# Seventeen instead of nineteen destination buckets as dense products in the first two graph convolution passes

## The reference: what is computed

```python
x = x + gnn0(layernorm(x), src, dst, edge_weight)   # one weighted neighbour sum
x = x + experts(layernorm(x))                       # top 2 of 8 feed-forward experts
x = x + convolutions(layernorm(x), src, dst)        # three layers, below
x = x + slice_attention(layernorm(x))               # 8 heads, 64 slices

def convolutions(x, src, dst):
    row, col = src and dst with a loop at every node
    norm = dinv[row] * dinv[col]                    # dinv = 1/sqrt(degree)
    for i in range(3):
        h = x @ W[i]
        h = segment_sum(h[row] * norm[:, None], col, 6250) + b[i]
        x = relu(layernorm(h) * gamma[i] + beta[i])
    return x
```

## Time and profile before

| | |
|---|---|
| median of three runs | 4934.6 us (4934.17 to 4947.35) |
| the profiled execution | 4942.1 us, span 4940.4 us |
| PE, DVE, ACT, POOL busy | 74%, 38%, 19%, 59% of the span |
| stage 1 | 97 to 1290 us |
| expert blocks | 1381 to 2190 us, PE busy 787 of 809 |
| pass 1, pass 2 | 767 us each, PE busy 619 and 621 |
| pass 3 | 919 us, PE busy 712 |

### The profile page before, as it was taken

One profiled execution on the slowest core, in us unless ns is written; L12 is line 12 of the kernel. 1 busy time (PEld: TensorE's weight loads), 2 busy tenths in 40 slices (PEclk: granted clock), 3 DMA queues, 4 the chain that ended last, 5 costly groups with the idle time before them and its releaser, 6 DMA issues. The chain is left out here.

```text
span 4940.4 us, 53616 instructions
## 1 busy us (share of the span) xinstructions
PE 3646.7 (74%) x17389; PEld 2837.0 (57%) x17389; DVE 1858.6 (38%) x6845; ACT 922.3 (19%) x2129; POOL 2931.6 (59%) x2861
## 2 busy tenths in 40 slices
PE   1455555555699999976788887778788787877768
PEld 1344444444488888865566665557566555555547
DVE  4344443444711111125233333133333255555564
ACT  1233333333122222214000001000000011111120
POOL 4666666666467777751566665666666565656520
PEclk6677777777799999988899998889899798998888
DMA  5444444444166666666565556556567454555423
GB/s 157 146 163 155 143 152 158 152 141 135 23 185 196 183 195 184 190 178 209 164 187 176 181 178 203 163 170 186 174 183 221 145 164 150 153 159 156 143 95 141
DMA packets 431741, 807.47 MB, mean 163 GB/s; under 512 B 112299, under 2 KB 263250, under 8 KB 430738
## 3 DMA queue, kind: packets, MB, share of 16 engines
q1 hardware_dynamic: 264274, 465.45, 28.7%
q0 software_dynamic: 164064, 331.94, 24.6%
q10 hardware_dynamic: 3168, 7.21, 0.4%
HBM read 670.69 MB, written 133.67 MB: 163 GB/s over the span
## 5 line engine op out<-in xcount | busy, mean ns | idle before, releaser
L2544 POOL DMA_INDIRECT rows_h<-table,step_src x1522 | 1465.9, 963 | 1096.4 <-issue 547.3
L2584 PE MATMUL bank_g<-X,piece_h 128*128 128x256 f32 x5194 | 1240.4, 390 | 51.1 <-issue 36.9
L2584 PEld LDWEIGHTS bank_g<-X,piece_h 128*128 128x128 f32 x5194 | 1018.8, 197 | 240.5 <-issue 97.1
L892 POOL DMA_INDIRECT rows_r<-table,step_src x782 | 743.9, 951 | 402.2 <-issue 210.7
L917 PE MATMUL bank_r<-rows_r,hots_r 128*128 128x257 f32 x1564 | 440.7, 434 | 468.1 <-ACT rows_r L902 329.4
L917 PEld LDWEIGHTS bank_r<-rows_r,hots_r 128*128 128x128 f32 x1564 | 321.7, 215 | 565.4 <-ACT rows_r L902 359.5
L1754 POOL DMA_INDIRECT kept_A<-one_d,place_d x296 | 466.4, 1576 | 90.5 <-issue 90.2
L928 DVE TENSOR_SCALAR hots_r<-lane,step_dst 128x128 f32<-128x128 f32 x782 | 209.7, 290 | 669.9 <-remote 434.6
L1864 PE MATMUL pH_e<-xe_e,w_e 128*128 128x256 f32 x1792 | 398.1, 380 | 1.2 <-DVE xe_e L1812 1.2
L1879 PE MATMUL pY_e<-w_e,h_e 128*128 128x256 f32 x1792 | 396.1, 379 | 0.0
L1864 PEld LDWEIGHTS pH_e<-xe_e,w_e 128*128 128x128 f32 x1792 | 341.9, 191 | 48.4 <-DVE xe_e L1812 1.6
(11 more groups left out here) (348 smaller groups left out, 3663.2 us busy)
## 6 DMA issues: line engine op xcount, KB each, us to landing
piece_h<-kept_A SPq DMA_DIRECT2D x371, 448.0 KB
w_e<-in_L_ffn_W SPq DMA_DIRECT2D x112, 1024.0 KB
kept_A<-zero_r SPq DMA_DIRECT2D x133, 448.0 KB
rows_h<-table,step_src POOLq DMA_INDIRECT x1522
got_c<-y SPq DMA_DIRECT2D x14, 896.0 KB, 8.0
kept_sw<-vec_g SPq DMA_DIRECT2D x49, 256.0 KB
rows_r<-table,step_src POOLq DMA_INDIRECT x782
table<-ACC SPq DMA_DIRECT2D x48, 256.0 KB
```

The costliest lines, as they stand in the source:

```text
L892: nc.gpsimd.indirect_dma_start(out=r["rows"][:, x, 0:D], out_offset=None, in_=r["table"][:, :], in_offset=bass.IndirectOffsetOnAxis(ap=c[" ...
L2544: nc.gpsimd.indirect_dma_start(out=d["rows"][:, x, :], out_offset=None, in_=tables[l - 1][:, :], in_offset=bass.IndirectOffsetOnAxis(ap=c[ ...
L2584: mm = pe.matmul(pD[o % 2][:, 0:D], d["piece"][:, n % AB, x % PC, :], c["X"][:, ORDER[x // PC] * PC + x % PC, :], start=(x == 0), stop=(x ...
```

## The change

WIDE has 17 buckets instead of 19, and its quota ends at step 750 instead of 754.

```diff
@@ -131,7 +131,7 @@
     return sum(1 for i in range(min(tiles, k // Q * Q + Q)) if i % ring // Q == x)
 
 
-WIDE, NARROW = Pass(19, 754, 3, 10), Pass(15, 744, 9, 14)
+WIDE, NARROW = Pass(17, 750, 3, 10), Pass(15, 744, 9, 14)
 PASSES = {1: WIDE, 2: WIDE, 3: NARROW}
 F, TD, FN, TM = WIDE.F, WIDE.TD, NARROW.F, NARROW.TD
 ED = TD * P
```

## The result

The changed kernel takes 5004.3 us (median of four runs, 5003.39 to 5020.65) against 4934.4 us (four runs): ratio 1.0148, 95% interval 1.0133 to 1.0164. It is slower, and the time is the one that was forecast (5004). Part of that hit is luck: the forecast stood on the profiled execution of the kernel before, 4942.1 us, 7.5 us above the median. The loss itself was forecast as 62 us and is 70 us between the medians and 61 us between the profiled executions. One step of the sum was wrong and others moved too.

A forecast was written before the change was run, and what follows sets the result against it. The prediction took POOL's gather stream to bound passes 1 and 2. To the profiled 4942.1 us it added 62 (31.2 a pass), all other terms 0 or left out: 5004 us; range 4895 to 5040, likeliest case 4962 to 5040.

The forecast's parts named there:

- The pacer: Passes 1 and 2: POOL's stream of gathers, not the busier PE, sets the pace; chance 0.72, 4962 to 5040 us.
- floor: Gather stream: a group of eight gathers takes at least 11.65 us, whatever the dense work on PE is.
- 11.65 is no floor: Sign of a wrong prediction: an interval under 11.5 us in a wide pass; the 1.76 us wait then belongs to PE.
- The gathers added: Wide passes: 32 more gathers, four groups a pass; 61 intervals for 57, +13.6 to +48.9 us a pass.
- The relief of TensorE: Wide passes: 98 fewer dense products make PE 37.5 us lighter a pass; wins back at most 0.58 us an interval.
- half: Share of the 0.58 us over 11.65 taken as won: 11.94 us an interval, +31.2 us a pass.
- The lag's cause: Node groups: PE, in order, waits for ScalarE's copies (4.54 us once); the ACT and DVE chains keep their length.
- The scatters: Experts' stage: 32 fewer scatters of counts, 50 us of POOL, covered by PE busy 787 of 809 us; worth 0.
- The switch of shapes: PE: four more visits to 128x32 lane products a pass, each draining TensorE; 1.7 us a pass at most, left out.
- TensorE as pacer: Rival, passes 1 and 2: PE sets the pace, each up to 37.5 us shorter; 4867 to 4905 us, chance 0.16.
- gathers absorbed: Rival, passes 1 and 2: POOL's 148 us of waits take in 40 us of new issue; 4942 us, chance 0.12.
- Nothing is won back: Rival, passes 1 and 2: the interval stays 12.23 us, +98, 5040 us; upper end of the likeliest case, no separate chance.

The follow-up runs named there:

- half_products_again: The kernel before with 399 of 931 dense products a pass left out in passes 1 and 2; 4863.1 us against 4943.0, ratio 0.9832.
- f21: The kernel before with 21 buckets instead of 19 in passes 1 and 2; 4321.9 us against 4330.2, ratio 0.9981.

## Why the prediction was right, and where it was not

*The pacer.* Right in what paces on the second chip, where it is shown: the pass follows the gathers, POOL issues without a wait and TensorE follows the rows by 4.2 us. On the first chip it came out right in the number, and the mechanism is shown in part only: the interval hardly depends on the dense work, but TensorE runs some 20 us behind the gathers, and POOL waits too. The 11.65 us a group, read from three stretches with different work on PE, is what pass 1 shows when 399 products are left out (11.67). But "floor" was too strong. The stretch of pass 3 was one with little node work; the whole pass averages 13.07 us a group. And "no stretch of some length goes under 11.57" doesn't hold in the same trace: seven groups take 80.5 us in pass 2 (3244.60 to 3325.12), 11.50 each, and 56 gathers of stage 1 76.8 us (105.27 to 182.06), 10.97 per eight. Nor is it the stream's own on every chip: on the second one a group takes 10.08 us, POOL's issue alone. The prediction's own sign for "11.65 is no floor" (an interval under 11.5) is met there; but what it was to mean, that the 1.76 us belong to PE, is not: there POOL has no such wait, whatever PE does.

*The gathers added.* Right: 61 intervals, 729.1 us after the fourth group, 728.3 forecast. The rest of a pass, forecast as unchanged, grew by 3.6 us in pass 1: 2.8 in the first fill (40.2 us to the fourth group where it was 37.5) and 0.8 in the drain (33.25 against 32.46).

*The relief of TensorE.* The size came out as taken, 0.28 of the 0.58 us an interval, but "half" was a choice between two ends, and its agreement with the first pair is luck as far as is known: pass 3, in which nothing was changed, moved by 0.11 us a group in the same pair, and stage 1's gathers by 0.13 the other way. That products left out bring the interval down to about 11.7 is shown (11.67 with 399 fewer); what 98 alone are worth on that chip was not tried. On the second chip it is 0.

*The lag's cause.* Only in part. I put TensorE's lag down to waits for ScalarE's copies, and took these as unchanged. The rows of the node groups' products in pass 1, before and after, say that about half of the idle time before ended so (45.6 of 93.6 us), and that the whole shrank to 31.9 us:

```profile
L2567 PE MATMUL bank_g<-w_g,xt_h 128*128 128x256 f32 x196 | 69.5, 516 | 93.6 <-issue 48.1 <-ACT xt_h L2712 45.6
```

```profile
L2567 PE MATMUL bank_g<-w_g,xt_h 128*128 128x256 f32 x196 | 55.3, 431 | 31.9 <-issue 23.3 <-ACT xt_h L2712 8.6
```

Pass 2 shows the same (93.0 and 39.7 us). Why they shrank, by fewer products or by the new places of the node groups, was not tried. The trace of the changed kernel, late in pass 1, shows another kind of stop, in a run of products that wait for nothing that the profile shows:

```profile
3076.45 1.06 PE L2602 MATMUL bank_g<-rows_h,hot_h 128*32 128x256 f32 x13
3077.77 0.40 PE L2602 MATMUL bank_g<-rows_h,hot_h 128*32 128x256 f32 x1 [0.26 <-issue]
3079.20 0.38 PE L2602 MATMUL bank_g<-rows_h,hot_h 128*32 128x256 f32 x1 [1.04 <-issue]
3080.60 0.38 PE L2602 MATMUL bank_g<-rows_h,hot_h 128*32 128x256 f32 x1 [1.02 <-issue]
3081.99 1.31 PE L2611 MATMUL bank_g<-mid_h,spread_h 128*128 128x256 f32 x2 [1.01 <-issue]
```

One matmul record in 1.4 us, several in a row, with the rows long there: these are the lane products of the 62nd group, whose last gather was issued at 3057.44. In pass 1 of the same program on the second chip, the dense products have no idle time before them but for the first piece (12.7 us); on the first chip they had 26.5 us more. The cause of these stops is open.

*The scatters.* Wrong. The step said that PE's 787 of 809 us cover them and that POOL "has room", worth 0. It was worth 14.4 us. The busy share misled: POOL's 631.54 us are instructions alone, and each of its 483 instructions has 0.30 us of issue behind it (145 us), which makes 776 of 809. And the block is the unit, not the stage: a block with five scatters was more than full (14.56 us of POOL beside 14.15 of TensorE), and the change takes such blocks from 47 to 15. The prediction saw the gain as bounded by PE's 22 idle us and then took 0; 12.6 of them were waits for exactly these gathers, of which 1.9 were left after.

*The rest.* Stage 1 was 13.2 us longer up to the experts. On the second chip this start is 1195.7 us with 19 buckets and 1194.5 with 17, so nothing there says that the change makes it; on the first chip that start is 1363.8 in the trace before and 1354.7 in half_products_again, with the same code up to there, so much of it is likely spread. Pass 3 to the end, 5.5 us shorter, and the stretch ahead of pass 1, 5.0 us shorter, have no cause that the runs tell; from pass 3 to the end half_products_again is 21.7 us shorter with unchanged code. So 5004 is in part a sum of errors that cancel: +73 in the passes where 62 was forecast, -14.4 of scatters, +13.2 in stage 1, -10.5 without a cause. The range has a flaw of its own: its lower end, 4962, adds to the median and its upper end, 5040, to the profiled execution.

*The switch of shapes.* Left out at 1.7 us a pass at most, from the idle time before the lane products. That idle time is no sign of a drain: in pass 1 of f21, where TensorE never waits for rows, it is 0.0 us before 908 lane records. What a switch costs inside the records no run shows.

*The rivals.* TensorE as pacer and gathers absorbed both fell. On the first chip no pass came under the 11.43 us that they needed (11.95 with the change, 11.67 with 399 products left out); on the second the length did not follow TensorE up to 19 buckets. That TensorE's own stops, rather than its products, share in the pace on the first chip is a rival that no run excludes. The rule of the Trainium skill (DMA: Bandwidth & Descriptors, Anatomy of one DMA) by which a gather of this size lands in an estimated 2.3 us stood behind the first of them. On the second chip the profile has 2.8 us from issue to landing for stage 1's gathers, near to it, and POOL indeed hardly ever waits there; what did not follow is that TensorE then becomes the pacer, because POOL's own issue does. Nothing is won back (5040) was not the case either.

## What to carry to other kernels

Where two streams must end together, find the pace of each in stretches where the other has little to do, and price a shift of work by the stream that paces; the busier engine may be the one that waits. Then look whether the other engine really waits for the pacer's output (4.2 us behind it on the second chip, 20 on the first): where it doesn't, something else holds both. Read an engine that issues transfers by its whole cycle, with the issue gap of every instruction, and by the unit that repeats (a block), not by its busy share over a stage: a stage can look covered while each of its blocks is full. Work that another engine's idle stage can hold is cheap to move: 56 scatters moved gave 17 us, and made room for the step from 19 to 21 buckets, 52 us in all.

## What the runs showed of the hardware that was not expected

The same program takes 4934 to 4943 us in one setting and 4325 to 4330 us in another (I said first and second chip, but number 2 stands beside both times). The gather instruction is as long on both (954 and 955 ns in pass 1), but on the first POOL waits ahead of most groups of eight, mostly with a releaser that the profile can't name (36 waits of 1.76 us in pass 1 before, 40 of 2.0 after), and TensorE stops for some 1.0 us between single products; on the second neither is seen with 17 buckets. The difference is in the waits: in pass 1 of the changed kernel 141.7 us of POOL's time on the first chip (80.5 + 61.2), none on the second. What makes them is open. The unnamed waits are not for the ring: in pass 1 of the kernel before, it had been free for a median of 4.9 us when they ended. Which edits help depends on the setting only in part: the change costs 1.015 in both.
